# A Sinkhorn chain of five rows with its products and sums on Pool and its reciprocals on the vector engine, in a decoder layer on one Trainium2 core

## The reference

```python
def sinkhorn_log(logits, num_iters=50, tau=0.1):
    Z = logits / tau
    def step(carry, _):
        u, v = carry
        u = -logsumexp(Z + v[..., None, :], axis=-1)
        v = -logsumexp(Z + u[..., :, None], axis=-2)
        return (u, v), None
    (u, v), _ = scan(step, (u0, v0), None, length=50)
    return exp(Z + u[..., :, None] + v[..., None, :])
...
H_res = sinkhorn_log(H_res_logits)         # a 4x4 matrix for each token
H_res = (1.0 - g) * I + g * H_res
x_mixed = einsum('btij,btjc->btic', H_res, x_streams)
y_distributed = einsum('btc,btn->btnc', y, H_post)
return (x_mixed + y_distributed).reshape(B, T, nC)
```

## Time and profile before

| what | value |
|---|---|
| median of 3 runs | 1185.0 us (1184.17 to 1185.19) |
| profiled execution: its own time | 1183.39 us |
| profiled execution: span of the core | 1181.6 us |
| PE busy | 1024.4 us, 87% of the span |
| DVE busy | 902.3 us, 76% |
| ACT busy | 612.5 us, 52% |
| POOL busy | 487.9 us, 41% |
| mean granted clock | 0.938 |

### The profile page before, as it was taken

The page is one execution under the profiler, slowest core; times in us unless marked ns, Lnnn a source line. Parts: engine busy times, 40 slices in busy tenths (PEclk is TensorE's granted clock), DMA queues, the critical chain, the costliest instruction groups (busy, mean ns, idle before and its releaser), DMA issues. The chain is left out here.

```text
span 1181.6 us, 23561 instructions
## 1 busy us (share of the span) xinstructions
PE 1024.4 (87%) x7954; PEld 777.0 (66%) x7954; DVE 902.3 (76%) x2830; ACT 612.5 (52%) x1801; POOL 487.9 (41%) x721
## 2 busy tenths in 40 slices
PE   5889999999999999999956999999988998732548
PEld 4667777777778777787745677777666666421325
DVE  6756876668766678666663788778999999999994
ACT  6624554445554355544564677777676664320414
POOL 0714433334333343323433576667666555101312
PEclk9989999999999999999969999999999999855769
DMA  9110111110111101110032123324222231107606
GB/s 377 46 43 35 44 60 60 42 51 27 60 60 60 41 19 60 60 60 26 25 128 108 54 76 113 94 82 129 78 93 76 77 93 47 41 23 280 215 1 179
DMA packets 47236, 95.73 MB, mean 81 GB/s; under 512 B 5952, under 2 KB 30400, under 8 KB 47168
## 3 DMA queue, kind: packets, MB, share of 16 engines
q1 hardware_dynamic: 46880, 94.65, 23.9%
q10 hardware_dynamic: 288, 0.26, 0.1%
HBM read 64.48 MB, written 27.26 MB: 78 GB/s over the span
## 5 line engine op out<-in xcount | busy, mean ns | idle before, releaser
L689 POOL TENSOR_TENSOR prob_G<-prob_G,rl 128x512 f32<-128x512 f32 x96 | 99.7, 1040 | 250.8 <-DVE rl L570 250.8
L436 ACT ACTIVATE prob_G<-prob_G,negm 128x128 f32<-128x128 f32 x384 | 148.8, 389 | 83.4 <-DVE negm L512 83.4
L291 PE MATMUL ps_qkv<-w_hi,xT_hi 128*128 128x512 f32 x384 | 156.1, 406 | 17.4 <-DVE prob_G L575 9.2
L292 PE MATMUL ps_qkv<-w_lo,xT_hi 128*128 128x512 f32 x384 | 150.8, 393 | 0.0
L293 PE MATMUL ps_qkv<-w_hi,xT_lo 128*128 128x512 f32 x384 | 150.7, 393 | 0.0
L365 PE MATMUL ps_qkv<-wo_hi,aT_hi 128*128 128x512 f32 x256 | 108.9, 425 | 0.0
L367 PE MATMUL ps_qkv<-wo_hi,aT_lo 128*128 128x512 f32 x256 | 102.9, 402 | 0.0
L366 PE MATMUL ps_qkv<-wo_lo,aT_hi 128*128 128x512 f32 x256 | 102.9, 402 | 0.0
L291 PEld LDWEIGHTS ps_qkv<-w_hi,xT_hi 128*128 128x128 f32 x384 | 72.6, 189 | 43.8 <-issue 21.0
L508 DVE TENSOR_TENSOR prob_G<-ps_s,mask 128x512 f32<-128x512 f32 x96 | 64.9, 676 | 43.9 <-PE ps_s L274 43.4
L537 DVE TENSOR_TENSOR xT_lo<-ps_t,xT_hi 128x512 fp32r<-128x512 f32 x16 | 11.1, 691 | 100.9 <-ACT xT_hi L475 100.9
(11 more groups left out here) (290 smaller groups left out, 2765.9 us busy)
## 6 DMA issues: line engine op xcount, KB each, us to landing
xin<-in_x SPq DMA_DIRECT2D x16, 512.0 KB, 3.2
xres<-in_x SPq DMA_DIRECT2D x16, 512.0 KB, 5.5
x<-xres SPq DMA_DIRECT2D x16, 512.0 KB, 2.7
c_xin<-x SPq DMA_DIRECT2D x16, 512.0 KB, 5.3
c_cin<-in_ctx SPq DMA_DIRECT2D x16, 512.0 KB, 4.5
c_b_xres<-x SPq DMA_DIRECT2D x16, 512.0 KB, 3.2
rows_x<-c_row SPq DMA_DIRECT2D x64, 128.0 KB, 2.3
m_xm<-rows_x SPq DMA_DIRECT2D x16, 512.0 KB, 8.6
```

The source lines that it names most:

```text
L291: nc.tensor.matmul(ps_qkv[:, n, :], xT_hi[:, k, :], w_hi[:, k, cols], start=k == 0, stop=False)
L292: nc.tensor.matmul(ps_qkv[:, n, :], xT_hi[:, k, :], w_lo[:, k, cols], start=False, stop=False)
L436: r = nc.scalar.activation(prob(g)[:, j, :], prob(g)[:, j, :], ACT.Exp, bias=negm[:, h:h + 1], accum_out=lsum[:, h:h + 1])
L689: nc.gpsimd.tensor_tensor(prob(g), prob(g), rl[:, g * GROUP:(g + 1) * GROUP].rearrange("p (j o) -> p j o", o=1).to_broadcast([P, GROUP, T] ...
```

## The change

Rows are split 7, 5 and 4. Chain a begins one body later and takes 36 steps in a body instead of 32. Chain b begins in body 13 and is a `PoolChain`: after its first eight steps POOL does the product and the sum of each half, the sum as two additions (pairs, then the pairs' sum), and DVE does only the reciprocal (`take_reciprocal`, a take below). POOL and DVE wait for each other in each half. POOL also does the two additions of a block's end. In the ending the takes stand between steps of chains a and c, and by the end of it 45 of 98 takes are issued and chain c stands at step 52. In the mixing phase DVE issues four steps of chain c between two takes (twelve at the block's end, and twelve between chain b's last take and its coefficients), and POOL puts one half between its other instructions, until all of chain a's diagonals are done. The logits of row 14 go to another bank, so that PE need not wait for them to be read before it turns row 15, and row 15 has its own tile for `rs`. The coefficients of chain a are copied before chain b's block end.

```diff
-ROWS_OF_CHAINS = (6, 7, 3)
+ROWS_OF_CHAINS = (7, 5, 4)
...
+HALVES = tuple(2 * n for n in BLOCK_ITERS)
+FIRST_HALVES = tuple(sum(HALVES[:n]) for n in range(len(HALVES)))
...
+class PoolChain(Chain):
...
+    def log_ready(self, act, k):
+        if k <= FIRST_LOGS:
+            act.wait_ge(self.step, log_after(k))
+            return
+        n, i = divmod(k - FIRST_LOGS - 1, BLOCK_LOGS)
+        if i < 2:
+            act.wait_ge(self.rec, sum(HALVES[:n + 1]) - 1 + i)
+        else:
+            act.wait_ge(self.added, 2 * n + 2)
...
+def parts_through(h):
+
+    return 3 * (h + 1) - sum(first <= h for first in FIRST_HALVES)
...
+def pool_half(pool, chain):
+
+    nc, h = chain.nc, chain.pooled
+    TT = nc.gpsimd.tensor_tensor
+    by_rows = h % 2 == 0
+    done = parts_through(h - 1)
+    if h in FIRST_HALVES:
+        pool.wait_ge(chain.logs, FIRST_LOGS + FIRST_HALVES.index(h) * BLOCK_LOGS)
+        src = chain.mat
+    else:
+        pool.wait_ge(chain.rec, h)
+        TT(chain.grid(chain.tmp), chain.grid(chain.mat), chain.over_i(chain.cb) if by_rows else chain.over_j(chain.ra),
+           ALU.mult).then_inc(chain.part, 1)
+        done += 1
+        pool.wait_ge(chain.part, done)
+        src = chain.tmp
+    if by_rows:
...
+        TT(to, of[:, :, :, 0:2], of[:, :, :, 2:4], ALU.add).then_inc(chain.part, 1)
...
+    pool.wait_ge(chain.part, done + 1)
+    TT(red, one, other, ALU.add).then_inc(chain.part, 1)
+    chain.pooled += 1
+
+
+def pool_block_end(pool, chain, n):
...
+    pool.wait_ge(chain.logs, FIRST_LOGS + n * BLOCK_LOGS + 1)
+    TT(chain.grid(chain.logm), chain.grid(chain.logm), chain.over_j(chain.lra), ALU.add).then_inc(chain.added, 1)
+    pool.wait_ge(chain.added, 2 * n + 1)
+    pool.wait_ge(chain.logs, FIRST_LOGS + n * BLOCK_LOGS + 2)
+    TT(chain.grid(chain.logm), chain.grid(chain.logm), chain.over_i(chain.lcb), ALU.add).then_inc(chain.added, 1)
+
+
+def take_reciprocal(dve, chain):
+
+    h = chain.taken
+    dve.wait_ge(chain.part, parts_through(h))
+    to = chain.ra if h % 2 == 0 else chain.cb
+    chain.nc.vector.reciprocal(to[:, :, :], chain.red[:, :, :]).then_inc(chain.rec, 1)
+    chain.taken += 1
...
+        early_logits = p_a[:, 0, 0:NLOG]
...
-        begun_in(7, one_a)
-        steps_to[7, 4] = ((one_a, 10),)
+        begun_in(8, one_a)
+        steps_to[8, 4] = ((one_a, 10),)
+        begun_in(13, one_b)
         at = 10
-        for b in range(8, B - 2):
-            if b == 12:
-                parts = {0: at + 2, 1: at + 7, 2: END[0], 3: END[1], 4: END[1] + 14}
+        for b in range(9, B - 1):
+            if b == 13:
+                parts = {0: END[0] - 3, 1: END[0], 2: END[1], 4: END[1] + 18}
...
-                parts = {0: at + 2, 1: at + 7, 2: at + 23, 4: at + 32}
+                parts = {0: at + 2, 1: at + 7, 2: at + 25, 4: at + 36}
...
+                    r = nc.tensor.matmul(early_logits if m < LAST else logits, x3T[:, i, :], w24_sb[:, i, :], start=i == 0, stop=i == KD - 1)
...
-                pe.wait_ge(lg_done, n)
...
                         beside(b, 4)
+                        if isinstance(b, int) and c == LAST and i % 2 == 1:
+                            take_reciprocal(dve, one_b)
...
+                            if i % 4 == 3:
+                                take_reciprocal(dve, one_b)
...
                 def fill(count):
-                    weave(dve, (one_b, one_b.issued + count), (one_a, min(END[2], one_a.issued + count)))
+                    for i in range(count):
+                        advance(dve, one_a, END[2], 1)
+                        if i % 2 == 1:
+                            take_reciprocal(dve, one_b)
...
                 residual(0)
-                fill(6)
+                fill(8)
                 residual(1)
-                fill(18)
+                one_b.taken_by_residual = one_b.taken
+                fill(8)
                 gate_logits(n - 1)
                 gate_max(n - 1)
                 fill(14)
                 gate_logits(n)
                 dve.wait_ge(lg_done, n + 1)
-                weave(dve, (one_c, FIRST), (one_b, one_b.issued + FIRST), (one_a, min(END[2], one_a.issued + FIRST)))
+                for i in range(FIRST // 2):
+                    weave(dve, (one_c, one_c.issued + 2), (one_a, min(END[2], one_a.issued + 2)))
+                    take_reciprocal(dve, one_b)
                 branch_in(n - 1)
                 gate_max(n)
-                weave(dve, (one_b, one_b.issued + 12), (one_c, one_c.issued + 12), (one_a, END[2]))
+                take_reciprocal(dve, one_b)
+                for i in range(4):
+                    weave(dve, (one_c, one_c.issued + 3), (one_a, min(END[2], one_a.issued + 3)))
+                    take_reciprocal(dve, one_b)
                 branch_in(n)
-                weave(dve, (one_b, one_b.issued + 22), (one_c, one_c.issued + 22), (one_a, END[3]))
+                take_reciprocal(dve, one_b)
+                while one_a.issued < END[2]:
+                    weave(dve, (one_c, one_c.issued + 3), (one_a, min(END[2], one_a.issued + 3)))
+                    take_reciprocal(dve, one_b)
+                weave(dve, (one_c, one_c.issued + 3), (one_a, END[3]))
+                take_reciprocal(dve, one_b)
...
+                if far and isinstance(b, int) and b >= B - 2:
+                    while one_b.pooled <= (one_b.taken_by_residual if b == LAST else 6):
+                        pool_half(pool, one_b)
...
+            copies(one_a)
             logs(one_b, FIRST_LOGS + 1, FIRST_LOGS + BLOCK_LOGS)
-            copies(one_a)
-            take_out(0, one_a.n)
+            take_out(0, ROWS_AHEAD)
             logs(one_c, FIRST_LOGS + 1, FIRST_LOGS + BLOCK_LOGS)
+            take_out(ROWS_AHEAD, one_a.n)
...
+            def both(to):
+
+                while one_c.issued < to:
+                    advance(dve, one_c, min(to, one_c.issued + (12 if one_b.taken == HALVES[0] else 4)))
+                    if one_b.taken < sum(HALVES):
+                        take_reciprocal(dve, one_b)
...
+            while one_b.taken < sum(HALVES):
+                both(one_c.issued + 4)
...
+            advance(dve, one_c, one_c.issued + 12)
             coefficients(one_b, lambda: advance(dve, one_c, one_c.issued + 1))
...
+            pool.wait_ge(const_in, 32)
+            pool.wait_ge(own_step, 2)
+            for first, to in post_parts:
+                post_part(first, to)
+                half()
+            for n in range(one_a.n):
+                for g in range(NS):
+                    half()
+                    if n == 0 and g == 0:
+                        pool.wait_ge(coef_step, COEFS)
+                        spread_ready(pool, one_a)
+                    row_diag(n, g)
+            while one_b.pooled < sum(HALVES):
+                half()
```

More of the change, by code:

```diff
@@ new lines, in parts_through @@
+def parts_through(h):
[16 more added lines that the diff above has]
+    if by_rows:
+        to = chain.pairs[:, :, :].rearrange("p b (i k) -> p b i k", i=NS)
+        of = chain.grid(src)
+        TT(to, of[:, :, :, 0:2], of[:, :, :, 2:4], ALU.add).then_inc(chain.part, 1)
+        one, other = to[:, :, :, 0:1], to[:, :, :, 1:2]
+        red = chain.red[:, :, :].rearrange("p b (i o) -> p b i o", o=1)
+    else:
+        to = chain.pairs[:, :, :].rearrange("p b (k j) -> p b k j", k=2)
+        of = chain.grid(src)
+        TT(to, of[:, :, 0:2, :], of[:, :, 2:4, :], ALU.add).then_inc(chain.part, 1)
+        one, other = to[:, :, 0:1, :], to[:, :, 1:2, :]
+        red = chain.red[:, :, :].rearrange("p b (o j) -> p b o j", o=1)
+    pool.wait_ge(chain.part, done + 1)
+    TT(red, one, other, ALU.add).then_inc(chain.part, 1)
+    chain.pooled += 1
@@ L1405, in log @@
                     for k in range(first, to + 1):
-                        act.wait_ge(chain.step, log_after(k))
+                        chain.log_ready(act, k)
                         chain.log(k).then_inc(chain.logs, 1)
@@ L1702, in body @@
                     pool.wait_ge(pool_step, PS * b + 4)
-                    if last:
+                    final = isinstance(b, int) and b == LAST
+                    if last and not final:
                         pool.wait_ge(lg_done, b)
-                    TT(rs[:], ms2[:], mhalf, ALU.pow).then_inc(rs_done, 1)
+                    TT(rs_last[:] if final else rs[:], ms2[:], mhalf, ALU.pow).then_inc(rs_done, 1)
             iterations(pool, body)
+            while one_b.pooled <= one_b.taken:
+                pool_half(pool, one_b)
 def mixing_phase(nc, row0, rows_x, rows_y, facts, chains, gate, sel, fold, out):
@@ L1863, in _ @@
                     bank_free(NS * (n + 1) - BANKS)
-                    for step, count in ((BASES[2] - 22, 3), (BASES[2] - 5, 2)):
-                        pe.wait_ge(one_b.step, step)
+                    for taken, count in ((sum(HALVES) - 6, 3), (sum(HALVES) - 1, 2)):
+                        pe.wait_ge(one_b.rec, taken)
                         for i in range(count):
```

(35 more changed lines are left out.)

80 lines of the change are left out of this document (40 added, 40 removed).

## The result

The changed kernel takes 1211.65 us (median of 4 runs, 1210.74 to 1213.86), the kernel before 1184.59 beside it on the same chip: a ratio of 1.0233, with a 95% interval of 1.022 to 1.0246. It is slower by 27 us. The profiled execution took 1211.58 us with a span of 1209.8. The forecast was 1213, with 1209.8 for the span. Two runs at a low granted clock, one of split_only (1255.01 us at 0.81) and one of the kernel before (1641.83 us at 0.59), are left out of all comparisons.

A forecast was written before the change was run, and what follows sets the result against it. The prediction took DVE's throughput in chain steps to set the end. Its terms, 2.5 + 2.3 + 14.2 + 12.0 - 2.2 - 0.6, summed to +28.2 us: span 1209.8, time 1213, range 1192 to 1232.

The forecast's parts named there:

- The price of a half: Chain b's half on GpSimd and VectorE: three instructions, waits and reciprocal, 1.42 us against 1.01 on VectorE before.
- short and long halves: Rivals on a half's length: short, 1.15 us, total 1194, chance 0.14; long, 1.65 us, total 1232, chance 0.13.
- Point 1, the bodies: Autocorrelation bodies before row 15's picks: chain a's later begin and seven rows in its steps, +2.5 us.
- Point 2, picks and scales: Row 15's picks and scales: takes between them spaced by a half, 7.7 us instead of 5.3, +2.3.
- Point 3, the ending: First product to the ending's last step: takes wait for halves, 61.7 us instead of 47.55, +14.2.
- The boundary: Waits between ending and mixing phase: 0.6 us less, since SP's last stores are out before DVE is done.
- Point 4, the mixing phase: Mixing phase up to chain b's coefficients: the 53 halves left set the pace, +12.0 us.
- Point 5, the tail: From chain b's coefficients to the end: nine rows instead of ten, chain c slightly late, -2.2 us.

The follow-up runs named there:

- split_only: Kernel before with only the chain sizes 7, 5 and 4 and the kernel after's begin plan, chain b all on VectorE: 1196.1 us.
- sum_twice: Kernel after with the last GpSimd addition of each half done twice, result unchanged: 1238.92 us, ratio 1.0464.
- split_right: split_only with ScalarE's mixing-phase order as in the kernel after and 12 instead of 24 steps woven ahead of row 15's branch: 1191.86 us.
- no_bank: Kernel after with row 14's logits back in the bank of row 15's, so TensorE waits for their read again: 1213.1 us.
- logs_last: Kernel after with ScalarE's logarithms of chain a's last block moved behind row 15's copy and outputs: 1206.15 us.
- product_mix: split_right with chain b's products on GpSimd in the mixing phase only, and one more step of chain c per six of chain b: 1200.52 us.
- sum_dve: Kernel after with only chain b's products on GpSimd, each sum being one VectorE reduction ahead of its reciprocal: 1211.18 us.

## Why the prediction came out right, point by point

**The price of a half.** Taken as 1.42 us, it is 1.355. The three instructions were priced well: 0.33, 0.28 and 0.23 predicted, 0.33, 0.25 to 0.27 and 0.22 measured. The hand-over from GpSimd to VectorE, for which no row stood, takes 0.04 and not 0.08, and two of the other waits 0.07; the reciprocal lasts 0.28 and not 0.26. That this latency sets the pace is shown by sum_twice. The other side of the comparison, "against 1.01 now", is a half of seven rows; with the change's own five rows it is 0.90 on VectorE (split_right), so a half costs 0.45 us more on two engines, not 0.4. Both price rivals, short and long halves, fall: VectorE's products are longer beside GpSimd, but GpSimd's half stays at 1.34 to 1.37 us beside them.

**Point 1, the bodies: +2.5 predicted, +2.4 measured** (picks begin at 1011.44 against 1009.05). split_right, with the same plan and no half on GpSimd, has +2.1 at the first product. In both cases the scatter of that mark among equal kernels, 2.8 us, is larger than what could confirm the working behind the number.

**Point 2, picks and scales: +2.3 predicted, +2.9 measured.** Picks and scales themselves take 7.57 us (7.7 predicted). Between them and the first product a take stands 1.92 us, and the first product's wait for TensorE is 0.75 instead of 1.63; that these two make up the remaining 0.7 is argued and not shown.

```profile
1026.66 0.28 DVE L880 RECIPROCAL chain_b_cb<-chain_b_red 128x20 f32<-128x20 f32 x1 [1.92 <-POOL chain_b_red L861]
```

**Point 3, the ending: 61.7 us predicted, 59.4 measured** (1027.68 to 1087.07), +11.85 instead of +14.2. The takes come 1.355 apart and not 1.42. Row 14's bank at 0 is confirmed by no_bank. But the prediction puts the whole growth down to takes of GpSimd's halves, and that is wrong: in split_right, with none of them, the ending up to its last step grows by 7.4 us (55.0 against 47.55). That these are the sizes' own steps, seven rows of chain a among them, over which the waits for halves lie in the kernel after, is argued and not shown.

**The boundary: -0.6 predicted, +6.4 measured.** This is the step that failed. The prediction reasoned from SP's stores alone ("SP's last stores are out before DVE is done") and didn't follow ScalarE's order, in which the logarithms of chain a's last block stand ahead of row 15's copy. logs_last shows it.

**Point 4, the mixing phase: 86.05 us predicted, 80.6 measured**, +6.6 instead of +12.0. Of the 5.45 us, 53 halves at 0.065 less give 3.4; the 28 with a diagonal product beside them, put at 1.45, run at 1.36, 28 x 0.025 beyond that, or 0.7. The remaining 1.3 I can't place on one row: VectorE's waits for GpSimd in this phase are 7.9 us in all, for the constant's landing (2.17) and the block end among them. The prediction's baseline hides how much the halves cost: with the same sizes on VectorE the phase is 67.4 us (split_right), 6.6 less than before, so the kernel after loses 13.2 us against that and not 6.6. product_mix shows that the sign is not a matter of the sums alone: with the products alone on GpSimd the phase was longer too.

**Point 5, the tail: -2.2 predicted, -1.9 measured.**

The sum of the points is 2.4 + 2.9 + 11.85 + 6.4 + 6.6 - 1.9 = 28.2, and +28.2 was predicted: the misses of 7.0 at the boundary and of 7.8 in points 3 and 4, with +0.6 in point 2, cancel. The mechanism, a half paced by its latency on two engines, was right and its price nearly so; that the total came out to the tenth is luck. By kernels, the way from before to after is 7.5 us for the sizes (split_right), 14.3 for GpSimd's halves and the orders that come with them (logs_last against split_right) and 5.5 for ScalarE's order at the boundary. None of the eleven kernels beats the kernel before. What stays open: how much of the ending's +3.9 us from split_right to logs_last is GpSimd's single delay at row 15's statistics (VectorE idle 4.31 us at 1046.88), which no run took away.

## What to carry to other kernels

The chain of small dependent steps was paid by its latency once it left the engine on which another chain filled the gaps: with five rows, a half was 0.90 us on VectorE beside chain c and 1.36 on two engines, though VectorE's work fell. Before work is moved for balance, write down the round of each engine and the latency of one turn; the longest of them was the pace in the kernels whose rounds are worked out above. sum_twice and sum_dve show how near VectorE's round lay to the latency (1.19 and 1.36 us), and in product_mix moving even one instruction of three made a half longer (1.01 us and more against 0.90). And when the order of one engine is changed, read the orders of all engines that feed its next barrier: one line in ScalarE's list cost 5.5 us here, and two savings on chain b were given back through ScalarE's outputs behind chain c's logarithms.

## What the runs showed of the hardware that was not expected

- The two directions of a hand-over differ: from GpSimd's end to VectorE's start 0.04 us (1128.51 to 1128.55), back 0.07 to 0.08 (1128.83 to 1128.90, 1127.46 to 1127.54).
- On VectorE, instructions of two interleaved chains start 0.11 to 0.19 us apart though each is shown with 0.16 to 0.27 (split_right, 1122.17 to 1123.97). Taking two instructions of twelve out of that stream and giving them to GpSimd made two halves longer, 2.03 us at best against 1.80.
- A two-operand product of 64 columns that VectorE begins while an instruction of GpSimd runs ends 0.07 to 0.10 us after that instruction, in all 25 cases of product_mix's mixing phase (it began 0.06 to 0.29 us behind that instruction's start). Begun 0.06 us behind the start of GpSimd's product it takes 0.34 us; begun 0.28 us behind that of a diagonal product (0.40) it takes 0.21, hardly more than the 0.19 of the one that began at 1126.57, before GpSimd's product of 1126.73. VectorE and GpSimd in product_mix:

```profile
1126.57 0.19 DVE L765 TENSOR_TENSOR chain_c_tmp<-chain_c_mat,chain_c_cb 128x64 f32<-128x64 f32 x1
...
1139.88 0.34 DVE L762 TENSOR_TENSOR chain_c_tmp<-chain_c_mat,chain_c_ra 128x64 f32<-128x64 f32 x1
1140.96 0.34 DVE L765 TENSOR_TENSOR chain_c_tmp<-chain_c_mat,chain_c_cb 128x64 f32<-128x64 f32 x1
...
1139.81 0.33 POOL L827 TENSOR_TENSOR chain_b_tmp<-chain_b_mat,chain_b_ra 128x80 f32<-128x80 f32 x1 [0.79 <-DVE chain_b_ra L789]
1140.90 0.33 POOL L827 TENSOR_TENSOR chain_b_tmp<-chain_b_mat,chain_b_cb 128x80 f32<-128x80 f32 x1 [0.76 <-DVE chain_b_cb L792]
```
